# A graph kernel's count stage: stationary operands of 128 columns, and ScalarE moving two and three groups of columns with one instruction

## What is computed

```python
x = _layernorm(x + _L0_gnn_ref(x, edge_index, ...))       # softmax over the edges of each dst, sum of alpha * h[src]
x = _layernorm(x + _L1_gnn_ref(x, edge_index, ...))       # sum of h[src] * norm
x = _layernorm(x + _L2_gnn_ref(x, ..., edge_index, edge_type_3))
x = _layernorm(x + _L3_gnn_ref(x, ..., edge_index, ...))
```

## Time and profile before

| | us |
|---|---|
| median of 3 runs | 2724.74 (2724.6 to 2725.46) |
| the profiled execution | 2725.16 |
| its span | 2723.3 |
| TensorE busy | 2103.4 (77%) |
| VectorE busy | 2161.7 (79%) |
| ScalarE busy | 1860.7 (68%) |
| mean granted TensorE clock | 0.89 |
| the count stage, in the span | about 58 to 461 |

### The profile page before, as it was taken

One profiled execution on the slowest core, in us unless ns is written; L12 is line 12 of the kernel. 1 busy time (PEld: TensorE's weight loads), 2 busy tenths in 40 slices (PEclk: granted clock), 3 DMA queues, 4 the chain that ended last, 5 costly groups with the idle time before them and its releaser, 6 DMA issues. The chain is left out here.

```text
span 2723.3 us, 90169 instructions
## 1 busy us (share of the span) xinstructions
PE 2103.4 (77%) x33923; PEld 1853.3 (68%) x33923; DVE 2161.7 (79%) x4355; ACT 1860.7 (68%) x3006; POOL 86.7 (3%) x137
## 2 busy tenths in 40 slices
PE   3999997698698698395938999489976989567544
PEld 3655554598598597394927999389875889566522
DVE  6999996788788788515078999899988999759943
ACT  5999997675775775202059999699969999445431
POOL 1111111000000000000000000000000000000000
PEclk8999998899899899697978999799988999788767
DMA  3354554342342341272722331333304332043100
GB/s 85 158 225 196 206 224 196 120 142 65 114 150 62 119 148 59 86 220 66 236 80 83 113 100 35 101 106 95 95 21 129 96 95 83 4 140 121 41 9 24
DMA packets 182241, 302.56 MB, mean 111 GB/s; under 512 B 6394, under 2 KB 158845, under 8 KB 181976
## 3 DMA queue, kind: packets, MB, share of 16 engines
q1 hardware_dynamic: 181191, 297.57, 33.0%
q0 software_dynamic: 800, 1.26, 0.2%
HBM read 214.26 MB, written 84.54 MB: 110 GB/s over the span
## 5 line engine op out<-in xcount | busy, mean ns | idle before, releaser
L430 ACT ACTIVATE stage<-ps 125x375 f32 x625 | 313.9, 603 | 38.1 <-PE ps L376 33.8
L331 DVE TENSOR_SCALAR col<-iota_col,window_col 125x376 bf16<-125x376 f16 x1250 | 310.0, 318 | 3.6 <-PE ps L376 3.6
L376 PE MATMUL ps<-col,lo 125*125 125x375 bf16 x1250 | 290.3, 345 | 17.5 <-DVE col L331 17.2
L931 ACT ACTIVATE r1amsk<-r1ad,r1thr 125x640 f16 x360 | 259.6, 816 | 0.1
L931 ACT ACTIVATE r2amsk<-r2ad,r2thr 125x640 f16 x360 | 259.6, 814 | 0.1
L931 ACT ACTIVATE r0amsk<-r0ad,r0thr 125x640 f16 x360 | 259.6, 814 | 0.1
L1004 PE MATMUL ps<-r1mv,r1asel 125*128 125x66 f16 x5000 | 244.4, 196 | 4.8 <-issue 3.5
L1004 PE MATMUL ps<-r2mv,r2asel 125*128 125x66 f16 x5000 | 242.7, 196 | 2.4 <-issue 1.3
L1004 PE MATMUL ps<-r0mv,r0asel 125*128 125x66 f16 x5000 | 242.8, 196 | 1.1 <-DVE r0asel L953 0.5
L376 PEld LDWEIGHTS ps<-col,lo 125*125 125x125 bf16 x1250 | 136.9, 139 | 144.5 <-DVE col L331 141.4
L1004 PEld LDWEIGHTS ps<-r1mv,r1asel 125*128 125x128 f16 x5000 | 227.4, 100 | 8.7 <-issue 4.0
(11 more groups left out here) (537 smaller groups left out, 4412.5 us busy)
## 6 DMA issues: line engine op xcount, KB each, us to landing
counts<-stage SPq DMA_DIRECT2D x75, 800.0 KB, 4.8
ct<-counts_all SPq DMA_DIRECT2D x75, 800.0 KB, 4.6
counts_all<-total SPq DMA_DIRECT2D x25, 800.0 KB, 7.3
g0ct<-counts_all SPq DMA_DIRECT2D x25, 800.0 KB, 4.7
g1ct<-counts_all SPq DMA_DIRECT2D x25, 800.0 KB, 4.6
g2ct<-counts_all SPq DMA_DIRECT2D x25, 800.0 KB, 4.6
r0ct<-counts SPq DMA_DIRECT2D x25, 800.0 KB, 4.7
r1ct<-counts SPq DMA_DIRECT2D x25, 800.0 KB, 5.3
```

What stands on the lines that cost most here:

```text
L331: ins = v.tensor_scalar(col1[:, b % OHS * WIN + w], K.iota_col[:], K.window_col[:, bass.ds(i * (P // DG) + b, 1), w], None, ALU.is_equal)
L376: ins = pe.matmul(K.ps[0:P, s, 0:GW], lo1[:, b, 0:P, w], col1[:, s * WIN + w, 0:GW], start=(w == 0), stop=(w == WIN - 1))
L430: act.activation(dst.rearrange("p a r h d -> p (a r h) d"), K.ps[0:P, b % OHS, 0:GW].rearrange("p (x d) -> p x d", d=DG), ACT.Copy).then_i ...
L931: act.activation(msk[:, s % 5, n], ad[:, bass.ds(g % 2, 1), h] .rearrange("p a (b d) -> p (a b) d", d=PAD), ACT.Sigmoid, bias=T.thr[:, 1, ...
```

## The change

Three things, all in `count_edges`:

- The stationary operands get 128 columns instead of 125: `lo1[:, b, :, w]` (its last three columns are masks of node places 125 to 127, which no edge has), and the unit matrix `ident16`. The accumulators have 128 partitions accordingly, and so have ScalarE's moves and copies. The branch `wide` is changed in the same way.
- ScalarE empties the five banks with two instructions instead of five: one for banks 0 and 1, one for banks 2 to 4. It waits until the last group of the instruction is counted, and adds 2 or 3 to `taken` at its end.
- `move_total` follows after the second of them, as before after the fifth move.

TensorE's and VectorE's order of work, GpSimd and the DMAs stay as they are.

```diff
@@ add_up
-                            ins = pe.matmul(K.ps[0:P, OHS + half, 0:(h1 - h0) * NB], K.ident16[0:P, 0:P],
-                                            stage[0:P, bass.ds(slot, 1), r, h0:h1, bass.ds(25 * q, 25)]
+                            ins = pe.matmul(K.ps[:, OHS + half, 0:(h1 - h0) * NB], K.ident16[:],
+                                            stage[:, bass.ds(slot, 1), r, h0:h1, bass.ds(25 * q, 25)]
@@ a group
-                                ins = pe.matmul(K.ps[0:P, s, 0:GW], lo1[:, b, 0:P, w], col1[:, s * WIN + w, 0:GW],
+                                ins = pe.matmul(K.ps[:, s, 0:GW], lo1[:, b, :, w], col1[:, s * WIN + w, 0:GW],
@@ move_total
-                        ins = act.activation(total[0:P, bass.ds(slot, 1), h0:h1, 25 * q:25 * q + 25]
+                        ins = act.activation(total[:, bass.ds(slot, 1), h0:h1, 25 * q:25 * q + 25]
                                              .rearrange("p a h d -> p (a h) d"),
-                                             K.ps[0:P, OHS + half, 0:(h1 - h0) * NB].rearrange("p (h d) -> p h d", d=NB),
+                                             K.ps[:, OHS + half, 0:(h1 - h0) * NB].rearrange("p (h d) -> p h d", d=NB),
@@ ScalarE's loop
-                    for b in range(P // DG):
-                        act.wait_ge(counted, i * (P // DG) + b + 1 + OHS)
-                        dst = stage[0:P, bass.ds(i % STAGES, 1), :, :, DG * b:DG * (b + 1)]
-                        act.activation(dst.rearrange("p a r h d -> p (a r h) d"),
-                                       K.ps[0:P, b % OHS, 0:GW].rearrange("p (x d) -> p x d", d=DG),
-                                       ACT.Copy).then_inc(taken, 1)
-                        if b - 1 in ADDED:
-                            move_total(i, ADDED.index(b - 1))
+                    for n in range(P // DG // OHS):
+                        for s0, s1 in ((0, 2), (2, OHS)):
+                            act.wait_ge(counted, i * (P // DG) + OHS * n + s1 + OHS)
+                            dst = stage[:, bass.ds(i % STAGES, 1), :, :, DG * (OHS * n + s0):DG * (OHS * n + s1)]
+                            act.activation(dst.rearrange("p a r h (s d) -> p s (a r h) d", d=DG),
+                                           K.ps[:, s0:s1, 0:GW].rearrange("p s (x d) -> p s x d", d=DG),
+                                           ACT.Copy).then_inc(taken, s1 - s0)
+                        move_total(i, n)
```

More of the change, by code:

```diff
@@ L391, in five_groups @@
                                 for w in range(SLOTS):
-                                    ins = pe.matmul(K.ps[0:P, s, 0:GW], lo_wide[:, w, 0:P], col1[:, w, 0:GW],
+                                    ins = pe.matmul(K.ps[:, s, 0:GW], lo_wide[:, w], col1[:, w, 0:GW],
                                                     start=False, stop=False, skip_group_check=True)
```

## The result

The changed kernel took 2791.78 us in the median (2788.49 to 2794.52, 4 runs), the kernel before 2725.1 us (2724.6 to 2736.67, 4 runs): a ratio of 1.0217, 95% interval 1.0176 to 1.0258. The forecast was 2782 us, slower, in a range of 2745 to 2804. The profiled execution took 2794.52 us (span 2792.7), 69.4 us more than that of before.

What follows compares the result with a forecast made beforehand. VectorE was taken to bound the kernel before. Legs and B made an iteration 5 x 2.20 + 6.97 = 17.97 us against 15.70; 25 x (17.97 - 15.70) = +56.8 us on 2725.16 gave 2782 us, range 2745 to 2804.

Steps and rivals of the forecast that it cites:

- the ring: Merged move waits for group 4, whose matmuls follow groups 2, 3 and `add_up`, which await the previous move: 3.59 us a turn.
- The legs: From the end of one three-group move to the start of the next: 2.20 us, bounds 2.10 to 2.28.
- B: ScalarE's merged move of groups 2, 3 and 4 of every five: 1.39 us in the mean, ends 1.13 and 1.8.
- Both branches: Two paths from B's end to the next B's start, equally long within what could be read; the longer counts.
- the one over g2: Path from B's end directly to group 2, then group 3, `add_up`, group 4 and ScalarE: 2.18 to 2.26 us.
- the totals' branch: Path from B's end through ScalarE's two `total` copies, then `add_up`, group 4 and ScalarE: 2.19, taken as 2.20 us.
- the hand-over to `add_up`: From the end of ScalarE's `total` copies to the start of `add_up`'s matmul: 0.13 us.
- crossing: ScalarE's five-element runs crossing a multiple of eight: 0.165 us per affected group, taken as kept in merged moves.
- Rival 1: The crossing price vanishes in a long ScalarE instruction: +23.8 us, 2749 us; chance 0.09.
- Rival 2: VectorE stays the bound, the ring staying within 3.14 us: 2725 us, 2708 at best; chance 0.08.
- Rival 3: TensorE's pauses drop its clock to 1.2 GHz: +220 us for a whole stage, perhaps 2850 us; chance 0.05.
- What would show it: Stage signs: VectorE's masks wait 70 us, ScalarE about 95 us for TensorE; TensorE's loads wait for ScalarE, no longer VectorE.

Runs made afterwards that it cites:

- e1: The kernel before with only the 128-column operands and accumulators, ScalarE's moves still single: 2725.28 us, ratio 1.0008 to before.
- e3: The changed kernel with the six `add_up` matmuls after group 4 of a turn instead of group 3: 2724.96 us, ratio 1.0005 to before.
- e7: e3 with TensorE adding the unit matrix in each group and GpSimd keeping one addition in place of four: 2711.03 us, ratio 0.9947 to before.
- e8: e7 with ScalarE's moves single again and `add_up` behind group 3: 2710.2 us, ratio 0.9950 to before.
- e2: The kernel before with only ScalarE's moves merged, operands still at 125 columns: 2794.39 us, ratio 1.0262 to before.
- e4: The changed kernel with the six `add_up` matmuls behind group 1 instead of group 3: 2866.58 us, ratio 1.0526 to before.
- e5: The changed kernel with the split turned round, groups 0 to 2 moved first, then 3 and 4: 2735.18 us, ratio 1.0038 to before.
- e6: The changed kernel with each group written at a multiple of eight elements, so no run of five crosses one: 2755.27 us, ratio 1.0108 to before.
- e9: The kernel before (single moves, 125 columns) with `add_up` behind group 1: 2800.48 us, ratio 1.0273 to before.

## Why the prediction was right, step by step

- *VectorE bounds the kernel before, the others have slack.* Right: e1 shortens TensorE's loads, e3 ScalarE's work, for nothing; e7 and e8 shorten VectorE's turn by 0.5 us an iteration and gain 25 x 0.5 = 12.5 us (14 and 15 measured).
- *The 128 columns cost and give nothing by themselves.* Right (e1). In the ring the shorter load is worth about 4 us, as e2's iteration shows.
- *The merged move closes a ring.* Right, and shown three ways: opened without touching a move (e3), lengthened (e4), its move shortened (e5, e6); each time the iteration came out within 0.2 us.
- *The legs, 2.20 us.* Mis-sized by 0.04 us: 18.42 less five Bs of 1.444 leaves 5 x 2.24, which is +5 us over the stage; read turn by turn in 90 turns from 100 us on, the mean is 2.24 too. Both branches are nearly as long as each other, as foreseen, and the longer one holds each turn. In three turns of five that is the one over g2, which starts 0.13 to 0.15 us after B's end where I had bounded it by 0.13: 2.22 us in the mean, and `add_up`'s matmuls start 0.63 us after g2. In the other two it is the totals' branch: the hand-over to `add_up`, 0.13 us by the one row I had, takes 0.17 to 0.20 there, which makes 2.27 us in the mean; in the second turn shown `add_up` starts 0.69 us after g2 (247.65 and 248.34). Why the hand-over has two lengths stays open.
- *B, 1.39 us.* Mis-sized by 0.05 us: 1.444 us, +6 us over the stage. Without any crossing it is 1.18 (e6) where I had 0.51 + 0.62 = 1.13, so the missing piece is in the long instruction itself and not in the crossing. It comes with the second group: e6's two-group move takes 0.863 us for 0.82, and the third adds 0.313 for 0.31. The crossing's 0.165 us is right: 1.35 and 1.51 us with one and two crossing groups. These two terms are the whole miss: +11 us on 56.8, against 68 measured by the iteration.
- *The crossing is charged for each run, not for each instruction.* The sum took this side, and the durations and e6 decide for it. The Trainium skill (SBUF — State Buffer, "Door 1: The DMA port swizzle") has 16-byte lines, with a penalty for each access that crosses to a new one; ScalarE's writes here agree, at 0.165 us for 75 crossing runs, in single and merged moves alike.
- *Rival 1, merging is cheap:* refuted, B is 1.44 us. *Rival 2, VectorE stays the bound:* refuted for the change, and true as soon as the ring is opened. *Rival 3, the clock:* refuted, 0.99 (the 2.4 GHz level) in the same window as before, though TensorE pauses 0.8 to 1.15 us in each turn. Two of its numbers don't follow: the idle stretch of 2.60 us that ends at 102.67 began at 100.07, not 99.9, and +220 us for a whole stage would give 2945, so the 2850 has no sum behind it.
- *What would show it.* VectorE's waits came out at 47 us for the 70 forecast; the busy time of its masks rose by 15 us beside that (324.7 us, 310.0 on the page of before). Single masks are nearly as long as they were (0.31 us away from GpSimd's additions). But in an unbroken chain they start 0.23 us apart, so that their records overlap, and each wait breaks the chain and lets some 0.08 us more count as busy: at 99 waits for the masks that is an estimated 8 of the 15 us. A sum of waits therefore understates what the engine lost. ScalarE's waits ahead of B are 99 us for 95. That the loads would no longer wait for VectorE was wrong as a reading: 75 us are put down to it, though the loads start 0.1 us behind a B's end (247.62 after 247.51) and the row of the matmuls names ScalarE.

## What to carry to other kernels

An instruction that empties several buffers frees the first only after the last has been filled and moved, so look for what the producer must do, in its own order, between the release and the last buffer; add up that ring and compare it with the pace of the engine that bounds the stage. Merging saves nothing while the merging engine has slack, and it is free only while the ring is shorter than that pace: here a ring of 2.9 us (as reckoned for e3) was free and one of 3.7 us cost 2.2%, the difference being where six matmuls stood in the program. Single moves are no protection: with the six matmuls still earlier, they closed a ring of 3.77 us (e9). The gain lay with the engine that never waited: half a microsecond an iteration less for VectorE gave 0.5% with either kind of move.

## What I had not expected of the hardware

- GpSimd's additions and VectorE's masks take turns. The rows below are from the kernel before; only their starts matter, as some stand for several records. While additions run, each mask starts 0.39 to 0.40 us after the one before, where 0.23 is usual, and the starts of both engines alternate. Four additions hold up four masks by 0.17 us each, which is the 0.67 us of the slow stretch; the one addition in e7 holds up one, by 0.18 us.

```profile
210.22 0.83 POOL L314 TENSOR_TENSOR stage<-stage,ident 125x125 f16 x2
210.30 0.86 DVE L331 TENSOR_SCALAR col<-iota_col,window_col 125x376 bf16<-125x376 f16 x2
210.62 0.43 POOL L314 TENSOR_TENSOR stage<-stage,ident 125x125 f16 x1
210.69 0.87 DVE L331 TENSOR_SCALAR col<-iota_col,window_col 125x376 bf16<-125x376 f16 x2
211.01 0.43 POOL L314 TENSOR_TENSOR total<-total,ident 125x125 f16 x1
211.09 0.93 DVE L331 TENSOR_SCALAR col<-iota_col,window_col 125x376 bf16<-125x376 f16 x3
```

- The first addition of a series can last longer than the 0.43 us of the others: 0.93 before and 0.91 in e7, where it started while VectorE built `lo1`, and 1.24 in e5, where it started among masks and ended once VectorE paused; in the changed kernel it took 0.42. That is why the three `stage` additions took 1.71, 1.21 and 2.02 us in before, the changed kernel and e5.
- A run of five f16 that crosses a multiple of eight elements costs ScalarE 0.165 us / 75 = 2.2 ns, about half of what its five elements cost (5 x 0.83 = 4.2 ns).
- The width in partitions made no difference: ScalarE's moves took 603 ns on 125 partitions and 604 ns on 128.
